# Fused LoRA SwiGLU kernel: the last gate/up step takes over part of the split work of the down stage, and loads are issued in another order

## The reference, cut to what matters

```python
gate = x @ Wg + (x @ Ag[idx]) @ Bg[idx]        # per sequence, idx in 0..7
up   = x @ Wu + (x @ Au[idx]) @ Bu[idx]
h    = silu(gate) * up                          # 64 x 64 x 2048
x    = x + (h @ Wd + (h @ Ad[idx]) @ Bd[idx])   # back to 512 columns
x    = x + einsum('bct,bcd->bdt', x, w1[idx])   # a 64 x 64 mix of each sequence
```

## Time and profile before

| | before |
|---|---|
| median of 3 runs (lowest to highest) | 1301.45 us (1300.89 to 1303.17) |
| profiled execution: its own time / its span | 1302.31 us / 1300.7 us |
| mean granted TensorE clock | 0.971 of full speed |
| PE busy | 1216.8 us, 94% of the span |
| DVE / ACT / POOL busy | 781.4 us (60%) / 525.4 us (40%) / 94.9 us (7%) |
| share of the chain that ended last: PE / SP's queue / DVE / DMA / ACT | 80% / 7% / 4% / 3% / 2% |

### The profile page before, as it was taken

The page is one execution under the profiler, slowest core; times in us unless marked ns, Lnnn a source line. Parts: engine busy times, 40 slices in busy tenths (PEclk is TensorE's granted clock), DMA queues, the critical chain, the costliest instruction groups (busy, mean ns, idle before and its releaser), DMA issues.

```text
span 1300.7 us, 22988 instructions
## 1 busy us (share of the span) xinstructions
PE 1216.8 (94%) x7104; PEld 1083.9 (83%) x7104; DVE 781.4 (60%) x1389; ACT 525.4 (40%) x999; POOL 94.9 (7%) x188
## 2 busy tenths in 40 slices
PE   3656999989999989999999999998999999999998
PEld 2545778878888878888878888888999999999997
DVE  4534666786667776667777667754444554445453
ACT  2423444454444454344454444434333333334332
POOL 1200110000110000000000000010112111211110
PEclk9777999999999989999999999998999999999999
DMA  3346776477665566757656777656555545554540
GB/s 140 106 144 220 196 211 201 140 207 213 183 180 163 153 187 202 200 151 190 169 160 180 196 212 208 188 167 190 147 168 175 153 142 163 177 151 148 160 131 36
DMA packets 114492, 221.33 MB, mean 170 GB/s; under 512 B 26434, under 2 KB 68546, under 8 KB 114370
## 3 DMA queue, kind: packets, MB, share of 16 engines
q1 hardware_dynamic: 106112, 198.80, 53.0%
q0 software_dynamic: 7392, 19.41, 4.7%
q10 hardware_dynamic: 866, 1.66, 0.3%
HBM read 173.62 MB, written 46.14 MB: 169 GB/s over the span
## 4 chain that ended last, share of the span: by engine, by line
PE 80%; SPq 7%; DVE 4%; issue 3%; DMA 3%; ACT 2%; DVEq 0%; ACTq 0%
PE ps L894 14%; PE ps L895 14%; PE ps L896 13%; PE ps L906 8%; PE ps L1005 5%; PE ps L1009 5%; PE ps L1013 4%; PE ps L1012 4%; PE ps L1007 4%; PE ps L1014 4%; SPq L201 4%; PE ps L923 1%; ACT xo_hi L370 1%; SPq L159 1%; DMA bq<-b_dram 1%
## 5 line engine op out<-in xcount | busy, mean ns | idle before, releaser
L894 PE MATMUL ps<-xo_hi,w_hi 128*128 128x512 f32 x896 | 360.8, 403 | 29.2 <-DVE v L684 13.4
L895 PE MATMUL ps<-xo_lo,w_hi 128*128 128x512 f32 x896 | 356.2, 398 | 0.0
L896 PE MATMUL ps<-xo_hi,w_lo 128*128 128x512 f32 x896 | 353.2, 394 | 0.0
L894 PEld LDWEIGHTS ps<-xo_hi,w_hi 128*128 128x128 f32 x896 | 171.8, 192 | 62.1 <-DVE v L684 16.1
L896 PEld LDWEIGHTS ps<-xo_hi,w_lo 128*128 128x128 f32 x896 | 171.2, 191 | 38.4
L906 PEld LDWEIGHTS ps<-t_st,bq 128*128 128x128 f32 x1024 | 158.1, 191 | 51.2 <-DMA bq<-b_dram 30.9
L895 PEld LDWEIGHTS ps<-xo_lo,w_hi 128*128 128x128 f32 x896 | 171.9, 192 | 26.6
L906 PE MATMUL ps<-t_st,bq 128*128 128x256 f32 x1024 | 165.0, 284 | 28.5 <-DMA bq<-b_dram 28.5
L604 DVE TENSOR_TENSOR w_lo<-wsum,w_hi 128x512 fp32r<-128x512 f32 x128 | 88.5, 692 | 143.7 <-ACT w_hi L370 143.7
L604 DVE TENSOR_TENSOR hl<-h_raw,hh 128x1024 fp32r<-128x1024 f32 x64 | 78.4, 1225 | 158.6 <-ACT hh L370 158.5
L1005 PE MATMUL ps<-wd_hl,hh 128*128 128x320 f32 x512 | 161.5, 315 | 7.5 <-DVE hl L604 4.8
(11 more groups left out here) (73 smaller groups left out, 1559.5 us busy)
## 6 DMA issues: line engine op xcount, KB each, us to landing
bq<-b_dram SPq DMA_DIRECT2D x1024, 64.0 KB, 2.2
raw<-packed SPq DMA_DIRECT2D x64, 512.0 KB, 5.4
h_dram<-h_f SPq DMA_DIRECT2D x64, 512.0 KB, 3.7
h_raw<-h_dram SPq DMA_DIRECT2D x64, 512.0 KB, 4.2
ad_raw<-a_d SPq DMA_DIRECT2D x64, 128.0 KB, 2.8
xs<-x POOLq DMA_DIRECT2D x16, 512.0 KB, 5.1
y_out_dram<-ys POOLq DMA_DIRECT2D x30, 256.0 KB, 3.4
xst<-xg SPq DMA_DIRECT2D x14, 512.0 KB, 6.4
```

The lines of the kernel that those rows point to most:

```text
L894: pe.matmul(bank, st[0], mv[0], start=start and kk == 0, stop=False, skip_group_check=True)
L895: pe.matmul(bank, st[0], mv[1], start=False, stop=False, skip_group_check=True)
L896: m = pe.matmul(bank, st[1], mv[0], start=False, stop=kk == 1, skip_group_check=True)
```

## The change

Step 63, the last one of stage one, is written out by hand for ACT and DVE instead of being the last turn of their loops, and split work of stage two is put between its instructions. The loops now run to step 62; within them nothing changes. On SP, `load_h(0)` and `load_h(1)` are issued in the turn of step 62, `load_h(2)` and `load_h(3)` in that of step 63, and the last h store is issued after `load_wd(11)` to `load_wd(15)`. The amount of work is the same. GpSimd's and PE's lists do not change.

```diff
 (SP)
-            load_h(0)
-            store_h(STEPS - 1)
-            load_h(1)
-            load_h(2)
+                if s >= STEPS - 2:
+                    load_h(2 * (s - (STEPS - 2)))
+                    load_h(2 * (s - (STEPS - 2)) + 1)
             for c in range(11, CH):
                 load_wd(c)
-            load_h(3)
+            store_h(STEPS - 1)
 (ACT; the loop before it now ends at step 62)
+            s = STEPS - 1
+            keep_p1(s)
             h_hi(0)
+            keep_p5(s)
+            wd_hi(7)
+            keep_u2(s)
+            wd_hi(8)
             ad_hi(0, 0)
-            for c in range(7, CH):
+            wd_hi(9)
+            wd_hi(10)
+            silu_1(s)
+            wd_hi(11)
+            h_hi(1)
+            silu_2(s)
+            wd_hi(12)
+            ad_hi(0, 1)
+            for c in range(13, CH):
                 wd_hi(c)
-                if c == 8:
-                    ad_hi(0, 1)
-                    h_hi(1)
             ad_hi(0, 2)
 (DVE; the loop before it now ends at step 62)
-            make_h2(STEPS - 1)
-            make_h1(STEPS - 1)
+            s = STEPS - 1
+            make_h2(s - 1)
+            make_h1(s - 1)
             h_lo(0)
+            wd_lo(7)
+            wd_lo(8)
+            make_c11(s)
             ad_lo(0, 0)
-            for c in range(7, CH):
+            wd_lo(9)
+            make_u3(s)
+            make_c22(s)
+            wd_lo(10)
+            make_c12(s)
+            wd_lo(11)
+            make_h2(s)
+            make_h1(s)
+            h_lo(1)
+            wd_lo(12)
+            ad_lo(0, 1)
+            for c in range(13, CH):
                 wd_lo(c)
-                if c == 8:
-                    ad_lo(0, 1)
-                    h_lo(1)
             ad_lo(0, 2)
```

More of the change, by code:

```diff
@@ L530, in _ @@
             hi(eye_r[:, :], eye_f[:, :])
-            for s in range(STEPS):
+            for s in range(STEPS - 1):
                 g, c = divmod(s, CH)
-                more = s + 1 < STEPS
                 first, last = c == 0 and g > 0, c == CH - 1 and g + 1 < GROUPS
-                if more:
-                    w_hi_raw(s + 1)
+                w_hi_raw(s + 1)
                 if s:
@@ L543, in _ @@
                     x_hi(g, 5)
-                if more:
-                    w_hi_sum(s + 1, 0)
+                w_hi_sum(s + 1, 0)
                 if last:
@@ L550, in _ @@
                     x_hi(g, 6)
-                if more:
-                    w_hi_sum(s + 1, 1)
+                w_hi_sum(s + 1, 1)
                 if last:
@@ L802, in _ @@
                     x_lo(g, 4)
[L803 to L806, removed]
+                for k in range(4):
+                    w_add(s + 1, k)
+                w_lo_raw(s + 1)
                 if first:
@@ L810, in _ @@
                     x_lo(g + 1, 0)
-                if more:
-                    w_lo_sum(s + 1, 0)
+                w_lo_sum(s + 1, 0)
                 if first:
@@ L816, in _ @@
                     x_lo(g + 1, 1)
-                if more:
-                    w_lo_sum(s + 1, 1)
+                w_lo_sum(s + 1, 1)
                 if 0 < s < PIECES:
```

## The result

The changed kernel takes 1290.95 us (median of 6 runs, 1288.79 to 1294.61) where the kernel before takes 1301.83 us (6 runs, 1300.74 to 1303.93). The medians are 10.9 us apart, against a forecast gain of 11.5 us and a forecast time of 1290.0. The ratio of the two kernels on record is 0.991, 95% interval 0.9896 to 0.9925; the ratios given here come with the record and are not always the quotient of the two medians, which would be 0.9916. The profiled execution has a span of 1289.2 us.

What follows compares the result with a forecast made beforehand. PE bounds the kernel, losing 11.59 us at the border of the two stages; SP's queue must come forward too. SP's 11.47 us, the later shift, counts: 1301.45 - 11.5 = 1289.95, say 1290.0; range 1288.5 to 1294.4.

Steps and rivals of the forecast that it cites:

- What the border is worth: Border of the two stages on PE: 11.59 us lost, 7.47 of idle time and 4.12 of slow matmuls and restarts.
- The clock term: Pair 0 after the border stalls: throttled clock and restarts cost 4.12 us; without that mechanism the time would be about 1294.0.
- h loads at no price: SP in step 62: h loads 0 and 1 issued near 840.6 land by 848.6 at worst, costing nothing.
- ACT and DVE in step 63: Added splits delay PE's copies at most 0.1 us, `make_u3` 0.43 and `make_c12` 0.70; PE loses nothing.
- The cover of 0.5 us: DVE in step 63: `make_u3` ends at 858.93, PE needs it at 859.44, leaving 0.5 us.
- The last store: End of step 63: last h store at 863.07 instead of 862.41, if chunk 11 lands by 859.4; landing taken as 4.3 us.
- rival 1: Chunk 11 lands up to 7.5 us after issue, delaying last store; SP becomes the bound; gain 7.1, time 1294.35; chance 0.19.
- SP's list: First `load_bd` 1.20 us after the store, 11.47 us forward; same list to `load_ad(2)`; stall before `lora_down(0,0)` 0.6 us.
- The sum: PE's shift 11.59 us, SP's 11.47; the later counts: gain 11.47, rounded 11.5, forecast time 1290.0.
- rival 2: SP's list to `load_ad(2)` stretches back, its DMAs waiting for ring space or data; time 1301; chance 0.03.
- rival 3: h load 0 lands late, ACT holds PE's copy in step 63; landing at 865 gives 1303; chance 0.02.
- Rival 4: DVE fillers make PE wait for `make_u3`; half a microsecond gives 1290.5; counted within the forecast's 0.74.

Runs made afterwards that it cites:

- experiment 4: Changed kernel with the four A-factor loads of pair 1 issued in step 62 instead of behind pair 0's B-factor loads; 1290.80 us, ratio 0.9912.
- experiment 7: Changed kernel with pair 1's A factors loaded in step 62 and h load 3 behind chunk load 11, 1290.64 us; changed kernel repeated beside it, 1291.93 us.
- experiment 1: Kernel before with only SP's part of the change, ACT and DVE as before; 1301.43 us against 1302.79, ratio 0.9994.
- experiment 8: Changed kernel with `wd_lo(10)` ahead of `make_u3` on DVE; read from the profile, one timed run of 1292.35 us.
- experiment 5: Changed kernel with h load 3 issued behind chunk load 11 instead of ahead of it; 1292.02 us, ratio 0.9921.
- experiment 6: Changed kernel with all four h loads in step 62; read from the profile, one timed run of 1287.95 us.
- experiment 9: Changed kernel with last Silu and h products ahead of chunk 11's split, last store ahead of chunk load 15; one timed run of 1293.87 us.
- experiment 3: Changed kernel with batch 0's h and A-factor splits moved back behind step 63's last Silu and h product; 1295.89 us against 1302.94, ratio 0.9941.
- experiment 2: Kernel before with h loads early and only batch 0 split in step 63, chunks 7 to 15 behind it; 1298.01 us against 1302.79, ratio 0.9965.

## Why the prediction was right, point by point

- **What the border is worth.** Worked out as 11.59 us for PE alone, and 0.48 on top if SP is out of the way: 12.07 to a PE without stalls. Measured in experiments 4 and 7: 12.30. The 0.2 are the slots: before, the LoRA matmul started 0.64 after the end of its predecessor's slot (906.29), of which the view shows 0.48. Right for this execution of the kernel before.
- **The clock term.** 4.12 of the 11.59 us were put down to slow matmuls. After the change the clock is 1.00 in pair 0 and the 32 tiles take 24.16 us, against 24.14 worked out. Right, and a price of the idle time alone, 1294.0 us, is excluded by 1290.95. But the term was read from one execution: about 1.2 of the 4.12 us did not come in experiment 1 behind the same stall. That the medians lie 10.9 us apart, near the profiles' 10.73, suggests that the kernel before mostly pays about this much; how often it does was not measured.
- **h loads at no price.** Right: no wait for h load 0 in any kernel, even with all four issued together.
- **ACT and DVE in step 63.** Shifted by 0.87 us, the forecast for `make_u3` is 857.37 and it ran at 857.32; `make_c12` 859.47 and 859.39. PE got its copies within 0.1 us of before. The cover of 0.5 us was 0.42 by experiment 8. Right.
- **The last store.** Forecast 1.77 us after the end of step 63, under the condition that chunk 11 lands by 859.4 (858.5 in this execution). It landed at 859.6. The term that was mis-sized is "I take 4.3 us: landing at 859.2, no delay": it was 5.58, and in six profiles with two h loads in front it was 5.4 to 5.8. What the prediction had listed as the sign of rival 1, ACT idle before a `wd_hl` split and the store moving with it, is what the trace shows. Without the delay the store stands at 1.70 to 1.71 (experiments 5, 6, 7, 9), so the working around the term was right and the term cost 1.0 us.
- **SP's list.** First B-factor load 1.20 us behind the store: measured 1.16. From there the list to the last `load_ad(2)` issue took 27.96 us, against 28.33 before; the lateness of the store reached PE one for one: between experiment 5 and the changed kernel the store moves by 1.06 us and the LoRA stall by 1.09. With the store where it was forecast the stall is 0.24, 0.4 less than the 0.6 worked out. In 9 the landing of the last DMA added to it.
- **The sum.** Forecast 11.47. With the store where it was forecast (experiment 5) it is 11.81, and the late store takes 1.08 of that: 10.73, and 10.88 in the second profile; 10.9 in the medians. Two misses partly cancel: SP's list was 0.3 us better than worked out, chunk 11 cost 1.1. That the measured time is within 1 us of the forecast owes those 0.3 us to luck, and 0.4 of the forecast's distance in time comes from the base, 1301.45 us in three runs and 1301.83 in six.
- **The rivals.** Rival 1 (chunk 11 late, SP the bound) is the mechanism that acted, part of its way: 5.6 us instead of its 7.5, without the stall of batch 1 and without the slow clock. Its own sum was a little off (by its terms PE stalls 2.5 us before the LoRA matmul, not 2), which leaves its gain of 7.1 about as it was. Rivals 2 and 3 did not occur. Rival 4 did not occur either; it needs one more instruction pair on DVE, as experiment 8 shows.

I would have come nearer by asking how much was still in front of chunk 11 when it was issued. The forecast weighed the two nearest rows and took a value nearer the fast one (4.3, between 2.9 and 7.4), for reasons that were argued, not read.

## What to carry to other kernels

When the stalls at a border go, look at what was released behind them: here SP's list of DMA issues, which an in-order engine reaches only after the last store, was late by almost as much as PE and took about 1.5 of the 12.3 us that were to be had. A wait for a DMA put ahead of an instruction on an in-order engine makes everything behind it as late as that DMA; price the landing by what is queued in front of it. And parts of such a change don't add: early loads alone brought 3.0 us (1.2 of them by the clock), batch 0 with early loads 4.5, chunks with early loads 7.0, all of them 10.7.

## What the runs showed of the hardware

- A 256 KB load from DRAM landed 2.5 to 2.7 us after issue with only a 512 KB store ahead, issued 4 us earlier; 3.8 to 3.9 with one 512 KB load more, 5.4 to 5.8 with two.
- The length of an idle stretch alone did not tell what the clock did. Those of 1.17, 1.33 and 1.43 us left it at full speed; one of 2.25 us was followed by matmuls at half of it. One of 2.71 us at the border was followed by 0.51 in the kernel before and by 1.00 in experiment 1. After 3.61 us in experiment 3 the clock was 1.00 for the first 1.15 us of matmuls and 0.50 in the stretch from 868 to 870.
- The tail moved with the clock. Between the last two output sums lay 4.59 us before, 4.66 and 4.46 in the changed kernel and 5.16 in experiments 1, 2, 4, 5 and 7, whose code there is the same; in 3, 6, 8 and 9 it was 4.47 to 5.06. The granted clock of the last 6 us was 0.50 to 0.58 where it took 5.16 and 0.61 to 0.78 elsewhere. The first row is of the kernel before, the second of the kernel with both shortenings:

```profile
1294.70:1300.70 6.00, 1.07 (x3) 0.49 (x3) 1.60 (x3) 0.63 (x1) 0.00 (x0) 0.70 0.19 73
```

```profile
1283.20:1289.20 6.00, 1.65 (x3) 0.83 (x3) 1.39 (x2) 0.35 (x1) 0.00 (x0) 0.50 0.12 44
```

  The last three mix matmuls stand behind an idle time of 2.17 us in both, at full speed in the first and at half in the second. So 0.5 us of what the better versions gained at the border was given back at the end, which belongs to none of their edits. What decides when the clock falls there was not found.
- Stage one, the same code in every kernel up to step 62, ended between 858.7 and 862.7 us in the profiles. That is more than most terms here, and why single spans could not be compared.
